# An attention and mixture-of-experts block on one core: another order of the last stretch, batch 1 decoded by halves, two output sums moved to VectorE, the weights' fold in three parts

## The reference, cut to what matters

```python
# x: (4, 512, 128) f32; H=256, M=64, E=8 experts, EH=128, K=2
h = layernorm(x)
q, k, v = h @ Wq + bq, h @ Wk + bk, h @ Wv + bv
a = softmax(q @ k.T / sqrt(128)) @ v              # per batch, 512 x 512
x = x + layernorm(a)
h = layernorm(x)
s = sigmoid(h @ W_enc + b_enc)                    # 256 wide
cont = s @ W_s2c + b_s2c                          # 64 wide
probs = softmax(cont @ Wr + br); top 2 of 8, weights made to sum to 1 -> gate
y_e = relu(cont @ W1[e] + b1[e]) @ W2[e] + b2[e]  # all 8 experts are computed
moe = sum_e gate[e] * y_e
dec = sigmoid(moe @ W_c2s + b_c2s) @ W_dec + b_dec
z = layernorm(dec) * ln_g + ln_b                  # called LN_DEC below
out = x + layernorm(z)                            # called LN_Z below
```

## Time and profile before

| | |
|---|---|
| median of 3 runs | 143.56 us (143.04 to 144.24) |
| the profiled execution's own time | 143.67 us |
| its span, first to last instruction | 141.6 us |
| PE busy | 122.2 us (86%) |
| DVE busy | 89.1 us (63%) |
| ACT busy | 64.0 us (45%) |
| POOL busy | 32.8 us (23%) |
| chain that ended last | PE 73%, DVE 11%, ACT 6%, issue 4%, POOL 3% |
| mean granted TensorE clock | 0.977 |

### The profile page before, as it was taken

One profiled execution on the slowest core, in us unless ns is written; L12 is line 12 of the kernel. 1 busy time (PEld: TensorE's weight loads), 2 busy tenths in 40 slices (PEclk: granted clock), 3 DMA queues, 4 the chain that ended last, 5 costly groups with the idle time before them and its releaser, 6 DMA issues.

```text
span 141.6 us, 2514 instructions
## 1 busy us (share of the span) xinstructions
PE 122.2 (86%) x828; PEld 80.0 (57%) x828; DVE 89.1 (63%) x377; ACT 64.0 (45%) x185; POOL 32.8 (23%) x64
## 2 busy tenths in 40 slices
PE   6989999999978999999998898999895999888000
PEld 2447787787546777544687664478362667536000
DVE  1867429788896648933444589915299930955393
ACT  0557666656626762033874600467713213314711
POOL 4453021134210232100000341032420300023352
PEclk9999999999999999999999999999999999999955
DMA  3568200000000089000002960000299497000012
GB/s 113 150 173 221 94 0 2 0 0 2 5 0 0 8 281 306 10 0 0 0 0 74 303 225 0 0 5 2 79 264 317 104 294 287 5 0 0 2 74 74
DMA packets 10428, 12.29 MB, mean 87 GB/s; under 512 B 2818, under 2 KB 5520, under 8 KB 10416
## 3 DMA queue, kind: packets, MB, share of 16 engines
q1 hardware_dynamic: 9694, 11.95, 27.2%
q10 hardware_dynamic: 722, 0.20, 0.6%
HBM read 11.03 MB, written 1.11 MB: 86 GB/s over the span
## 4 chain that ended last, share of the span: by engine, by line
PE 73%; DVE 11%; ACT 6%; issue 4%; POOL 3%; POOLq 1%; DVEq 0%
PE ps_o L754 11%; PE ps_s L729 10%; PE ps_t L862 10%; PE ps_t L741 5%; PE ps_s L841 5%; PE ps_c L889 4%; POOL rstd L390 3%; DVE gated L1158 3%; PE ps_t L680 3%; PE ps_o L780 3%; PE ps_a L712 2%; PE ps_c L877 2%; PE ps_c L841 2%; DVE z L1187 2%; PE ps_a L702 2%
## 5 line engine op out<-in xcount | busy, mean ns | idle before, releaser
L390 POOL TENSOR_TENSOR rstd<-var_eps,minus_half 128x2 f32<-128x2 f32 (+1 forms) x32 | 24.9, 785 | 96.2 <-DVE var_eps L1057 42.3
L1081 DVE TENSOR_REDUCE neg_max<-ps_s 128x1 f32<-128x512 f32 x16 | 10.9, 689 | 13.5 <-PE ps_s L729 13.4
L754 PE MATMUL ps_o<-v,probsT 128*128 128x128 f32 x128 | 17.4, 279 | 1.4 <-ACT probsT L483 1.4
L862 PE MATMUL ps_t<-gated,w 128*64 128x256 f32 x128 | 17.8, 393 | 0.9 <-DVE gated L1158 0.8
L754 PEld LDWEIGHTS ps_o<-v,probsT 128*128 128x128 f32 x128 | 15.7, 191 | 4.2 <-ACT probsT L483 3.4
L729 PE MATMUL ps_s<-xnT,yT 128*128 128x512 f32 x32 | 16.3, 605 | 0.3
L478 ACT ACTIVATE probs<-ps_s,neg_max 128x512 f32<-128x512 f32 x16 | 11.0, 686 | 10.5 <-DVE neg_max L1081 10.4
L862 PEld LDWEIGHTS ps_t<-gated,w 128*64 128x64 f32 x128 | 7.7, 136 | 9.8 <-DVE gated L1158 5.1
L1158 DVE SCALAR_TENSOR_TENSOR gated<-ps_s,b_minus,gate_all 128x512 f32<-128x512 f32 x16 | 11.2, 743 | 0.5 <-PE ps_s L841 0.5
L483 ACT ACTIVATE probsT<-ps_t 128x512 f32<-128x512 f32 x16 | 9.5, 593 | 3.8 <-PE ps_t L741 3.6
L741 PE MATMUL ps_t<-ident,probs 128*128 128x128 f32 x64 | 9.8, 276 | 1.4 <-ACT probs L478 1.4
(11 more groups left out here) (175 smaller groups left out, 212.7 us busy)
## 6 DMA issues: line engine op xcount, KB each, us to landing
gate_all<-gates SPq DMA_DIRECT2D x32, 256.0 KB, 5.3
x_in<-in_L_attn_x SPq DMA_DIRECT2D x3, 256.0 KB, 3.5
w<-in_L_ffn_W SPq DMA_DIRECT2D x3, 256.0 KB, 3.8
out<-x_out SPq DMA_DIRECT2D x3, 256.0 KB, 2.0
x_in<-in_L_attn_x SPq DMA_DIRECT2D x2, 128.0 KB, 2.6
out<-x_out SPq DMA_DIRECT2D x2, 128.0 KB, 1.7
w_enc<-in_L_ffn_W_enc SPq DMA_DIRECT2D x1, 128.0 KB, 2.9
w_dec_raw<-in_L_ffn_W_dec SPq DMA_DIRECT2D x1, 128.0 KB
```

The lines of the kernel that those rows point to most:

```text
L390: nc.gpsimd.tensor_tensor(rstd[part], var_eps[part], minus_half[:, t0:t1], ALU.pow).then_inc(g_rstd[n], 1)
L754: mm = nc.tensor.matmul(attn_out(t), probsT[:, b % 2, t, k], v[:, b % 2, k], start=(k == 0), stop=(k == T - 1))
L862: mm = nc.tensor.matmul(ps_t[h * M:(h + 1) * M, 0:SH], w2[:, e], gated[:, e, h * SH:(h + 1) * SH], start=False, stop=(e == E - 1))
L1081: nc.vector.tensor_reduce(neg_max[:, b % 2, t:t + 1], ps_s[:, t % 2], AX_X, ALU.max, negate=True).then_inc(v_max, 1)
```

## The change

It changes the order of steps on every queue, and some steps themselves:

- Start: seven warm-up matmuls instead of nine. SP issues the first half of x, Wq, the second half of x, Wv and bv; ScalarE issues bq, bk and Wk. The fold of Wq and Wk waits for these two alone, the biases have a semaphore of their own. The fold is three steps: `fold_qk`, `fold_a`, and `fold_v`, which stands between the two halves of `turn_x(0)`. The statistics of batch 1's x are two steps around two row maxima, `turn_x(1)` comes two steps later.
- Batch 2's attention: `exps(2, 0)` ahead of `values_out(2)`; `router_top` is cut in two (`router_index` apart), for batch 0 with two row maxima between.
- Batch 3's attention: `decode(0, 2)` and `(0, 3)` behind `turn_probs(3, 2)`, `hidden_pair(1, 0)` ahead of `attend(3, 3)`.
- Last stretch: `encode(3, ...)` ahead of `decode(1, ...)`, which is done by halves, the first into the bank `ps_t`, the second into `ps_c`; its scaling, squares and variance are by halves too. The pair of experts 4 and 5 comes before that of 2 and 3 in batch 2. On VectorE the z of batch 1 goes behind the gating of batch 2, and four gated tiles of batch 3 stand ahead of `dec_scale(2, 0)`.
- Output of batches 0 and 2: centring and sum are on VectorE (eight instructions a batch), and `z_norm`, `minus_means` and GpSimd's `z_add` remain for batch 1 alone; `store(0)` and `store(2)` wait for VectorE.
- `decode` adds its bias with one matmul for each part instead of one for each tile.

```diff
-WARM_UP = 9
+WARM_UP = 7
...
+            if n == LN_DEC and b == 1:
+                return HALVES
...
+        def decoded_bank(b, t):
+
+            if b == B - 1:
+                return ps_a if t >= TH else ps_t
+            return ps_t if b == 1 and t < TH else ps_c[:, 0]
+
         def decoded(b, t):
 
-            if b == B - 1 and t >= TH:
-                return ps_a[:, t * P:(t + 1) * P]
-            return (ps_t if b == B - 1 else ps_c[:, 0])[:, t * P:(t + 1) * P]
+            return decoded_bank(b, t)[:, t * P:(t + 1) * P]
...
-            for i, (t0, t1) in enumerate(HALVES):
-                sp.dma_start(x_in[:, 0, t0:t1], x_dram[0, :, t0:t1]).then_inc(d_x[0][i], 16)
+            sp.dma_start(x_in[:, 0, 0:TH], x_dram[0, :, 0:TH]).then_inc(d_x[0][0], 16)
+            sp.dma_start(w_qkv[:, 0], Wq).then_inc(d_qk, 16)
+            sp.dma_start(x_in[:, 0, TH:T], x_dram[0, :, TH:T]).then_inc(d_x[0][1], 16)
+            sp.dma_start(w_qkv[:, 2], Wv).then_inc(d_wv, 16)
+            sp.dma_start(bv_row[:, :], row(bv)).then_inc(d_wv, 16)
...
-                if b < B - 1:
-                    sp.wait_ge(g_out, b + 1)
+                if b == 1:
+                    sp.wait_ge(g_out, 1)
                 else:
-                    sp.wait_ge(v_out, t1)
+                    sp.wait_ge(v_out, T * (b // 2) + t1 + (T if b == B - 1 else 0))
...
-            for b in range(3):
-                if b >= 1:
-                    inverse_std(LN_DEC, b, 0)
-                inverse_std(LN_Z, b, 0)
-                minus_means(b)
-                if b < 2:
-                    z_add(b)
+            inverse_std(LN_Z, 0, 0)
+            inverse_std(LN_DEC, 1, 0)
+            inverse_std(LN_DEC, 1, 1)
+            inverse_std(LN_Z, 1, 0)
+            minus_means(1)
+            z_add(1)
+            inverse_std(LN_DEC, 2, 0)
+            inverse_std(LN_Z, 2, 0)
             inverse_std(LN_DEC, B - 1, 0)
             inverse_std(LN_DEC, B - 1, 1)
-            z_add(2)
...
-            for i, weight in enumerate((Wq, Wk)):
-                act.dma_start(w_qkv[:, i], weight).then_inc(d_qk, 16)
             for i, bias in enumerate((bq, bk)):
-                act.dma_start(b_qk[:, i:i + 1], bias.rearrange("(d a) -> d a", a=1)).then_inc(d_qk, 16)
-            act.dma_start(w_qkv[:, 2], Wv).then_inc(d_wv, 16)
-            act.dma_start(bv_row[:, :], bv.rearrange("(a d) -> a d", a=1)).then_inc(d_wv, 16)
+                act.dma_start(b_qk[:, i:i + 1], bias.rearrange("(d a) -> d a", a=1)).then_inc(d_qk_bias, 16)
+            act.dma_start(w_qkv[:, 1], Wk).then_inc(d_qk, 16)
             act.wait_ge(g_warm, 1)
...
             second_exp(0)
+            exps(2, 0)
             values_out(2)
             for b in range(2):
                 n, m = b + 1, b + 2
                 more = m + 1 < B
-                exps(m, 0)
                 if b >= 1:
+                    exps(m, 0)
                     for c in range(HC):
...
-            for c in range(HC):
-                spike2(1, c)
+            spike2(1, 0)
             hT_out(3)
             second_exp(2)
-            z_norm(0)
+            spike2(1, 1)
+            spike(3, 0)
+            spike(3, 1)
             gate_out(2)
             dec_square(1, 0)
-            spike(3, 0)
-            spike(3, 1)
             cont_out(3)
+            dec_square(1, 1)
             second_exp(3)
             gate_out(3)
-            z_norm(1)
             moe_out(2)
             for c in range(HC):
                 spike2(2, c)
+            z_norm(1)
             dec_square(2, 0)
             moe_out(3)
             for h in range(2):
                 for c in range(HC):
                     spike2_last(h, c)
-            z_norm(2)
...
+            def fold_v():
                 pe.wait_ge(d_wv, 32)
...
+            def fold_a():
                 pe.wait_ge(a_wqk, 2)
...
+                if b == 2:
+                    pe.wait_ge(a_c2s, HC * b)
...
+                elif b == 2:
+                    pe.wait_ge(v_z1, parts_done(LN_DEC, 1, 0))
+                    pe.wait_ge(a_dec_square, T + TH)
...
-                nc.tensor.matmul(decoded(b, t), ones_bf[:, :], b_dec_stack[:, :], start=True, stop=False)
+                last = any(t == t1 - 1 for _, t1 in parts(LN_DEC, b))
+                for t0, t1 in parts(LN_DEC, b):
+                    if t == t0:
+                        nc.tensor.matmul(decoded_bank(b, t)[:, t0 * P:t1 * P].rearrange("p (t d) -> p t d", d=D),
+                                         ones_bf[:, :], b_dec_stack[:, :].unsqueeze(1).to_broadcast([P, t1 - t0, D]),
+                                         start=True, stop=False)
                 for c in range(HC):
                     mm = nc.tensor.matmul(decoded(b, t), spikes2[:, b % 2, c, t * P:(t + 1) * P], w_dec[:, c],
-                                          start=False, stop=(c == HC - 1))
-                if any(t == t1 - 1 for _, t1 in parts(LN_DEC, b)):
+                                          start=False, stop=(last and c == HC - 1))
+                if last:
...
-            fold_weights()
-            turn_x(0)
+            fold_qk()
+            fold_a()
+            turn_x(0, 0)
+            fold_v()
+            turn_x(0, 1)
...
-            turn_x(1)
             scores(0, 2)
             turn_probs(0, 1)
+            turn_x(1)
...
                 scores(m, 3)
-                if b >= 1:
-                    decode(b - 1, 2)
-                    decode(b - 1, 3)
                 attend(m, 1)
                 turn_probs(m, 2)
                 if more:
                     turn_x(m + 1)
+                if b >= 1:
+                    decode(b - 1, 2)
+                    decode(b - 1, 3)
                 attend(m, 2)
                 turn_probs(m, 3)
                 if more:
                     project_y(m + 1)
-                attend(m, 3)
-                hidden_pair(b, 0)
+                    attend(m, 3)
+                    hidden_pair(b, 0)
+                else:
+                    hidden_pair(b, 0)
+                    attend(m, 3)
                 hidden_pair(b, 1)
                 if more:
                     project_v(m + 1)
...
             turn_h(3)
             hidden_pair(2, 0)
-            for t in range(T):
-                decode(1, t)
-            turn_gates(2)
             encode(3, 0)
             encode(3, 1)
+            turn_gates(2)
+            decode(1, 0)
+            decode(1, 1)
             to_cont(3)
+            decode(1, 2)
+            decode(1, 3)
+            route(3)
+            hidden_pair(2, 2)
             hidden_pair(2, 1)
-            route(3)
             expert_biases(2)
-            hidden_pair(2, 2)
             turn_gates(3)
...
+            def z_centre(b):
+                for t in range(T):
+                    nc.vector.tensor_scalar(zn[:, b % 2, t], z[:, b % 2, t], mean_var[:, LN_Z, b % 2, t, 0:1], None,
+                                            ALU.subtract).then_inc(v_zn, 1)
+
+            def z_add(b, i):
+                dve.wait_ge(g_rstd[LN_Z], parts_done(LN_Z, b, i))
+                for t in range(*parts(LN_Z, b)[i]):
+                    if b < B - 1:
+                        dve.wait_ge(v_zn, T * (b // 2) + t + 1)
+                    else:
+                        dve.wait_ge(a_zn, T + t + 1)
+                    nc.vector.scalar_tensor_tensor(x_out[:, b, t], zn[:, b % 2, t], inv(LN_Z, b, t),
+                                                   x_mid[:, b, t], ALU.mult, ALU.add).then_inc(v_out, 1)
...
-            x_stats(1)
+            x_stats(1, 0)
             row_max(0, 0)
             row_max(0, 1)
+            x_stats(1, 1)
             x_norm(1)
...
             z_stats(0, 0)
-            z_means(0, 0)
             router_top(2)
+            router_index(2)
             router_gates(2)
+            z_centre(0)
+            z_add(0, 0)
             dec_scale(1, 0)
+            dec_scale(1, 1)
+            router_top(3)
+            router_index(3)
+            router_gates(3)
+            for e in range(4):
+                gate_hidden(2, e)
             dec_var(1, 0)
+            dec_var(1, 1)
+            for e in range(4, E):
+                gate_hidden(2, e)
             z_stats(1, 0)
             z_means(1, 0)
-            router_top(3)
-            router_gates(3)
-            for e in range(E):
-                gate_hidden(2, e)
-            gate_hidden(3, 0)
-            gate_hidden(3, 1)
+            for e in range(4):
+                gate_hidden(3, e)
             dec_scale(2, 0)
-            for e in range(2, E):
-                gate_hidden(3, e)
+            gate_hidden(3, 4)
+            gate_hidden(3, 5)
             dec_var(2, 0)
+            gate_hidden(3, 6)
+            gate_hidden(3, 7)
             z_stats(2, 0)
-            z_means(2, 0)
+            z_centre(2)
+            z_add(2, 0)
```

(20 more changed lines are left out.)

42 lines of the change are left out of this document (20 added, 22 removed).

## The result

The changed kernel takes 138.39 us (137.38 to 140.34, median of 4 runs), the kernel before 143.9 in the same comparison: ratio 0.9602, 95% interval 0.9491 to 0.9713. A second comparison of the same kernel gave 0.9597, interval 0.9562 to 0.9633. That is inside the range of 134.7 to 139.2, 2.0 us above the forecast of 136.4, and above the narrower band of 135.9 to 137.3 that the forecast had. Ratios leave out executions over 1.5% longer than the fastest of the same kernel; medians do not.

A forecast was written before the change was run, and what follows sets the result against it. TensorE was taken as the bound (73% of the chain of waits), plus a 10.6 us tail; 0.5 + 1.05 + 0.75 + 1.6 + 0.7 + 2.7 = 7.3 off 143.67 gave 136.4 us, range 134.7 to 139.2.

The forecast's parts named there:

- A: Start: fewer warm-ups and an earlier Wk let the fold begin near 4.6 us; gain 0.5 us.
- D1: Experts of batch 2: earlier routing of batch 3, limited by landings of the gates' broadcast; gain 1.6 us, bounds 1.0 and 2.4.
- B: Batch 2's first softmax: TensorE's 1.36 us wait for exponentials goes, a 0.45 wait follows; gain 1.05 us.
- C: Batch 3's attention: two 0.69 us waits for probsT filled, cut by a 0.6 wait for gated tiles; gain 0.75 us.
- D2: Experts of batch 3: four gated tiles precede decode(2), the 0.38 us wait goes; gain 0.7 us, bounds 0 and 0.9.
- E: Tail after the last product: ScalarE squares at once, no GpSimd sum beside the variance; gain 2.7 us, bounds 2.0 and 3.0.
- Rival 4: Slower: fewer warm-ups and TensorE's stops at the start keep its clock low; 145.5 us if until 17 us; chance 0.03.
- rival 2: Gains half realised: reordered stretches meet unseen waits; 138.0 to 139.7 us; chance 0.26.
- if the fold's matmuls show the lower level past 6 us: Sign at the start that the prediction is wrong: TensorE's fold still at the lower clock level after 6 us.
- 1, broadcasts that don't bind: Experts of batch 2: store out of the way, tiles early, so gain there is 2.4, total 135.6 us; chance 0.15.
- 3, shared ports: Tail: GpSimd's root waits 1.1 us for VectorE's z_centre, costing 0.7; 137.1 us; chance 0.05.
- 5, no effect: Tail bound by the store and roots alone; 142 to 144 us; chance 0.03.

The follow-up runs named there:

- the old start: Changed kernel with the whole start as before the change (nine warm-ups, old load order, one fold), the rest changed: 137.05 us, ratio 0.9516.
- tail edit: On the old start, batch 2's output back on ScalarE (z_norm ahead of batch 3's squares) and GpSimd's sum: 139.23 us, ratio 0.9670.
- both edits: On the old start, batch 0's first-half store behind broadcast 3 and batch 3's gates written from ScalarE's queue: 136.39 us, ratio 0.9496.

## Why the prediction was right, and where it was off

The sign and the range were right, and four of the six terms came near their size; two were mis-sized, A and D1. Profile against profile:

| part | predicted | measured | what the runs show |
|---|---|---|---|
| A start | 0.5 | 0.16 | none at the end; the new start costs 0.8% |
| B batch 2's softmax | 1.05 | 0.85 | wait 0.48 for 1.36, as forecast 0.45 |
| C batch 3's attention | 0.75 | 0.75 | B and C undone: waits of 1.75 back |
| D1 experts of batch 2 | 1.6 | 0.8 | broadcast 2 holds 1.0 |
| D2 experts of batch 3 | 0.7 | 0.7 | the wait of 0.38 at 121.89 is gone |
| E tail | 2.7 | 2.9 | 1.5 by the moved output (an edit), 1.3 by VectorE's order (read from the rows) |

That the median of 138.39 lies in the range says little for the sum, because the start adds long executions that the prediction had only in a rival. With the old start the median is 137.05, and without the broadcast of batch 2 it is 136.02: so the start and the landings together cover the 2 us that were missing.

**A, mis-sized.** I took the fold's first matmul for the path. "Gain 0.5 to 0.9 less what the clock costs" was nearly met at that matmul, 0.43. But behind it the product waits 0.72 for ScalarE's copies, and the transposes and `project_y` then follow TensorE's own work; of 0.43 there was 0.27 at the scores. The fold itself did not run at the lower level: its four matmuls took 0.68 from 4.83 on, where the working had 1.0. Rival 4 named a clock at its lower level, with the stops as its reason, and put 1.5 on a rise 2 us late, which I counted in rival 2. The trace shows a fall instead, after the level had risen, in one of two profiles of this kernel; it costs 1.3 there. I had looked for it at the fold ("if the fold's matmuls show the lower level past 6 us"); it came near 7.7. It does not account for the longest executions, as said above, so why the new start costs 0.8% stays open in part.

**B and C, right** in place and size: what is late next was the copy of probsT (0.48), and for C the gated tiles behind the variance (0.52; 0.6 was predicted, against 1.38 of waits removed). The "1.75" from which the prediction starts in C has no row; its own 0.75 comes out of 1.38 less 0.6.

**D1, mis-sized.** The times of the working, shifted by the 1.75 us won earlier, were met where VectorE decides: logits at 101.08 (102.8 predicted without the shift), first gated tile at 103.72 (105.4). The step that failed is the allowance for the transfers: 0.5 for a store ahead of them, and nothing for how the landings spread. The store does delay the issue by some 0.55, but with it away the kernel gains nothing, and without the broadcast it gains 1.0. From the earlier trace rows I had the first and the last landing, 3.3 and 5.8, but put tiles "105.6 to 111.2" in a smooth row; they run as the landings come, with 0.51 and 0.77 between, and these land on TensorE as 0.85.

D1 is also no fixed number. From the start of batch 1's `to_spikes` to that of batch 2's it is 22.01 us before and 21.16 in the changed kernel. In the seven other profiles of kernels with the same steps there it is 20.36 to 21.62, so D1 was worth 0.4 to 1.65 in them; without the broadcast it is 19.86, worth 2.15. The predicted 1.6 lies at the top of what the landings allow.

The order itself holds tightly: z of batch 1 put back ahead of the logits, alone, costs 5.3. TensorE's next pair writes the logits' bank, before the change as after it. Before, an encode, `to_cont` and a hidden pair stood between batch 1's decode and the routing and covered VectorE's z, and the wait was 0.24; now nothing stands there. So 5.3 is no price against the kernel before. Broadcast 3 was right: predicted near 111.1, which is 109.35 less the shift of 1.75, and it came at 109.39.

**E, right in sum.** The prediction gave 2.4 to ScalarE's freed 1.65 us and 0.3 to GpSimd's sum. The tail edit shows 1.53 for the two together. The rest is that z of batch 2 starts 0.8 ahead of the last product's end (122.33 against 123.11), and started 0.5 behind it before (126.93 against 126.42): 1.3. Before, z waited 1.13 for the root of its decoder variance, which stood behind all gated tiles; now the variance stands two tiles earlier, at 120.25, and z waits for nothing. No edit tests this half.

**Rivals.** 1, broadcasts that don't bind: no, they bind by 1.0. 2, gains half realised: 138.0 to 139.7 is where the median lies, so by the median this rival describes the outcome as well as the forecast does. Its mechanism does not: no reordered stretch met an unseen wait of size apart from the landings, and the rest is the start's spread. 3, shared ports: no. The root at 124.93 took 1.01 beside four centrings of VectorE that ran from 124.76 without a gap. The Trainium skill, page "GPSIMD Engine Reference", section 8 (Key points), says that GpSimd contends with VectorE's instructions in a two-port mode or with two SBUF inputs; the trace doesn't show it for this instruction. 4 is answered under A. 5, no effect: no.

## What to carry to other kernels

After moving work on one engine, look for what another engine may write only once that work is done: one read put behind 2.5 us of other work and its root stopped TensorE for 4.3 us and cost 5.3 in the end. A start should be judged at the first dense stretch and over several executions, not at its first matmul; 0.43 us there came to nothing, and the kernels with this start spread by 3%. A wait for landings varies from one execution to the next, so a gain that runs into them needs more than one profile. Once an order is tight, bound what is left by leaving a transfer out (1.0 us here) before tuning its place in a queue.

## What was not expected of the hardware

- TensorE's granted clock fell to 0.50 near 7.7 us in one execution, for 3.4 us, and stayed at 1.00 in another of the same kernel with the same rows up to 7.5. TensorE had worked 3.17 us, stopped 0.47, worked 0.68, stopped 0.71 and then worked on. What made the difference is not shown. After a stop of 4.34 us it was 0.50 for over 6 us of dense work (105.8 to 112).
- A 16 KB write sent while a 2 MB broadcast was under way took 4.3 us from SP's queue and 4.9 from ScalarE's (4.3 in the kernel with both edits); with no broadcast, 1.5. The Trainium skill, page "DMA: Bandwidth & Descriptors", section "Queues, rings and completion order", says that a DMA engine takes turns between the queues for which it has work, packet by packet. The trace agrees as far as packets of both queues ran side by side from 107.7 to 109.8. If it is read to mean that the second queue gets ahead of a broadcast under way, these runs don't show that.
- The eight landings of one broadcast lay 3.2 to 6.4 us behind their issue in the changed kernel and 3.1 to 5.8 with the old start, the DMA engines 0.57 busy at 104 to 106 us in the first. What spreads them stays open; the broadcast holds the end by about 1 us in all.
- Four centrings with a mean took VectorE 0.87, less than the 1.1 of four normalisations.
